# Cross-attention of a decoder layer: the order of a step, the grouping of the routing, and where the token scatters are issued

## The chip, the cores and the metric

One core of a Trainium2 chip runs one whole decoder layer. The metric is the device time in microseconds. The engines are TensorE (PE), VectorE (DVE), ScalarE (ACT), GpSimd (POOL) and SyncE (SP), which here only issues DMAs.

## The reference, cut to what matters

x is 16 sequences of 128 tokens, width 512; 16 heads of 32.

```
x1  = x + self_attention(layernorm(x))
d   = rs * (softmax(q(layernorm(x1)) . k(ctx) / sqrt(32), masked) . v(ctx) @ Wo.T + bo)
d   = (d - mean(d)) / sqrt(var(d) + 1e-5) * gamma + beta        # rs = clip(residual_scale, 0, 0.3)
x3  = x1 + d
xf  = layernorm(x3)
scores = softmax(xf @ gate.T)             # 64 experts in 8 groups; best 3 groups, of them best 6 experts
slot = expert * 192 + min(position of the token among those of its expert, 191)
out = x3 + sum_k weight_k * expert_k(xf) + shared_expert(xf)
```

A token beyond place 191 of its expert shares the last slot; the last token of the expert that got there holds it.

## The kernel before, in words

Four phases follow each other, with a barrier of all engines between them: self-attention, cross-attention (`cross_phase`), the routed experts, the shared expert. Only `cross_phase` and its helpers are changed.

**The work of the cross-attention.** One step t handles one sequence (a tile of 128 tokens). A quad is four tiles. All matrices are split in a high and a low part (`_hi`, `_lo`), and `matmul3` (L35) adds three products per chunk, so one projection unit is 12 matmuls of 512 columns. A quad has four key units, four V units (one per tile) and four query units; `cross_units` (L646) spreads the units of the next quad over four steps, three per step. ScalarE copies the key and query units out of PSUM, VectorE the V units. `cross_fresh` (L658) says which x tiles are turned in a step, `cross_context` (L666) which context tiles are split.

**A step**, in PE's order: scores of tile t (`scores`, L1484), the spreading of the inverse row sums of tile t-1 over the columns (`widen`, L1519), unit 0, transposes of x, unit 1, transpose of xf (`turn_final`, t-2), output projection (`project_out`, t-1), router logits (t-2), positions of a group, unit 2, row sums (`sums`, t) and V products (`attend_v`, t). VectorE: bound the scores in four pieces (`bounded`), with `attn_out(t-1)` (V products times inverse) between the second and third; units, statistics; `output(t-1)`; the row maximum of the logits; `delta(t-1)` (writes x3); the group's routing; `final_norm(t-1)` (writes xf); `row_sums(t)` (reciprocal). ScalarE: four exponentials, the copy of the spread inverse (`rinv_out`), the high part of the attention (`attn_hi`), unit copies, the high part of xf, the contexts' high parts, the router exponential. POOL: the low part of the attention (`attn_lo`, L960), the contexts' low parts, the addition of beta to the residual tile (`residual`), the inverse deviations of the next x tiles (`inv_std`), of the delta and of x3 (`delta_factor`, `final_rstd`), and the scatters.

**PSUM.** Two banks `pj` take the units and the output projection in turn. Two banks `ex` are shared by the small products; `cross_uses` (L680) writes down their order of use, and each use waits until the one before was read: `ex[1]` holds in turn the spread inverse, turned x, the logits, the positions and the row sums.

**Routing.** After the router, VectorE ranks the experts of a group of tiles (`rank_experts`, L1280), chooses six per token (`choose_experts`, L1308), and, after PE's running counts, computes the slots (`place_tokens`, L1334). `CROSS_GROUPS` (L642) has six groups of 4, 4, 3, 3, 1 and 1 tiles; `group_steps` (L674) gives their steps. Then POOL writes each token's number to its slots in a table in DRAM: `scatter` (L979) issues six indirect DMAs of 128 numbers per tile. `SCATTER_STEP` (L643) gives the step of each tile; the scatters stand at the end of POOL's step. The expert phase reads this table first, after the last scatter and a last small store (L930).

**Start-up.** The first six weight pieces were loaded during the self-attention. SP (from L898) loads contexts 0 and 1, three x tiles, the mask, contexts 2 and 3 (each waits for the low part of the context two before, in a ring of two buffers), then weights, x tile 3, weights, contexts 4 to 7. ScalarE's queue issues the seven loads of biases and vectors (L1051 to L1056). POOL waits for all seven (L1022), scales `bias_q`, then makes the low parts of contexts 0 to 3 with the inverse deviations of x tiles 0 to 3 between them, then `constants` (L987), then the low parts of contexts 4 to 7. PE turns one x tile after each of the four first key units, so x tile 3, which needs the buffer of tile 0, can be loaded after the first one.

In the loop SP issues, per step, the loads of x and contexts, the store of x3(t-1), the store of xf(t-1), and the load of the residual tile t+1 (`load_xr`, L882).

## Time and profile before

| | us |
|---|---|
| median of 3 runs | 1815.17 |
| lowest, highest | 1814.08, 1817.7 |
| the profiled execution | 1820.86 |
| its span, first to last instruction | 1819.1 |

| engine | busy us | share of the span |
|---|---|---|
| PE | 1556.5 | 86% |
| DVE | 1229.8 | 68% |
| ACT | 897.3 | 49% |
| POOL | 672.4 | 37% |

The time to predict is the median; the rows are those of the one profiled execution, and times in them count from the start of its span. "Busy" is the union of the instructions of an engine; a wait is shown before the instruction that waited, with what ended it. DMA issues stand under SPq or ACTq.

### The profile page before, as it was taken

What the parts mean: (1) busy time and instruction counts of PE and PEld (TensorE: products, weight loads), DVE (VectorE), ACT (ScalarE), POOL (GpSimd) and SP (SyncE); (2) the same over time, 40 slices, a digit from 0 to 9 for tenths busy, and PEclk for the clock granted to TensorE, in tenths of its full rate; (3) what the DMA queues carried; (4) which work ended last, traced back from release to release, by engine and by line L of the source; (5) the groups of instructions that cost most, each with busy time, mean ns of one, the idle gap of its engine ahead of it and who ended that gap; (6) DMA issues with size and microseconds to landing.
All of it is one profiled execution on the core that took longest, in us unless ns stands there. A gap on an engine that the chain in (4) does not pass through costs nothing. (4 is left out here: it accounts for less than half of the span.)

```text
span 1819.1 us, 30976 instructions
## 1 busy us (share of the span) xinstructions
PE 1556.5 (86%) x10503; PEld 1311.8 (72%) x10503; DVE 1229.8 (68%) x2130; ACT 897.3 (49%) x1748; POOL 672.4 (37%) x925
## 2 busy tenths in 40 slices
PE   5999987588878855309999999999999999799996
PEld 3788865477767644208888888888888888577774
DVE  5677664455666664527888888888888888454455
ACT  3566653333323221007777777777777777411110
POOL 1222221323226355553433444433333333323563
PEclk9999998799989976659999999999999999899998
DMA  5012111422113010029777777777777775424663
GB/s 179 18 42 76 36 36 35 144 71 69 53 53 51 27 47 24 18 91 349 260 256 258 252 253 261 256 256 250 261 253 248 262 253 206 154 70 146 200 185 104
DMA packets 110493, 275.71 MB, mean 152 GB/s; under 512 B 17696, under 2 KB 17792, under 8 KB 110416
## 3 DMA queue, kind: packets, MB, share of 16 engines
q1 hardware_dynamic: 88848, 222.65, 35.9%
q0 software_dynamic: 18464, 50.45, 8.7%
q10 hardware_dynamic: 3104, 1.58, 0.3%
q8 instruction: 48, 0.79, 0.2%
q14 instruction: 29, 0.24, 0.1%
HBM read 232.59 MB, written 42.04 MB: 151 GB/s over the span
## 5 line engine op out<-in xcount | busy, mean ns | idle before, releaser
L1784 POOL TENSOR_TENSOR e_hid<-e_h_raw,e_hid 128x192 fp32r<-128x192 f32 (+1 forms) x192 | 177.9, 926 | 410.9 <-ACT e_hid L1840 409.5
L1998 PE MATMUL e_gu<-e_xT_hi_lo,e_wg 128*128 128x384 f32 (+1 forms) x768 | 231.0, 357 | 2.1 <-issue 1.1
L1998 PE MATMUL e_gu<-e_xT_hi_lo,e_wu 128*128 128x384 f32 (+1 forms) x768 | 229.8, 355 | 0.0
L2000 PE MATMUL e_gu<-e_xT_hi_lo,e_wu 128*128 128x192 f32 (+1 forms) x768 | 193.5, 252 | 0.0
L2000 PE MATMUL e_gu<-e_xT_hi_lo,e_wg 128*128 128x192 f32 (+1 forms) x768 | 193.3, 252 | 0.0
L1911 DVE TENSOR_TENSOR e_total<-e_gu,e_low 128x384 f32<-128x384 f32 (+1 forms) x192 | 106.1, 553 | 105.7 <-ACT e_low L1835 105.7
L39 PE MATMUL e_dn<-e_wd,e_hid 128*96 128x512 f32 (+1 forms) x384 | 154.2, 402 | 0.1
L41 PE MATMUL e_dn<-e_wd,e_hid 128*96 128x512 f32 (+1 forms) x384 | 151.5, 395 | 0.0
L40 PE MATMUL e_dn<-e_wd,e_hid 128*96 128x512 f32 (+1 forms) x384 | 150.5, 392 | 0.0
L1998 PEld LDWEIGHTS e_gu<-e_xT_hi_lo,e_wg 128*128 128x128 f32 (+1 forms) x768 | 138.1, 180 | 7.3 <-DVE e_total L1911 1.3
L2000 PEld LDWEIGHTS e_gu<-e_xT_hi_lo,e_wg 128*128 128x128 f32 (+1 forms) x768 | 140.2, 183 | 1.5
L1998 PEld LDWEIGHTS e_gu<-e_xT_hi_lo,e_wu 128*128 128x128 f32 (+1 forms) x768 | 138.0, 180 | 3.4
L2000 PEld LDWEIGHTS e_gu<-e_xT_hi_lo,e_wu 128*128 128x128 f32 (+1 forms) x768 | 140.2, 183 | 0.0
L1899 DVE TENSOR_TENSOR e_wu<-e_raw_u,e_wu 128x1408 fp32r<-128x1408 f32 x64 | 127.6, 1994 | 0.1
L1904 DVE TENSOR_TENSOR e_wd<-e_raw_d,e_wd 128x1024 fp32r<-128x1024 f32 (+1 forms) x128 | 120.5, 941 | 0.0
L2160 POOL DMA_INDIRECT h_yk<-y_dram,h_idx x96 | 104.0, 1083 | 28.0 <-issue 24.1
L1840 ACT ACTIVATE e_hid<-e_h_raw 128x192 fp32r<-128x192 f32 (+1 forms) x192 | 69.2, 360 | 90.3 <-DVE e_h_raw L1920 90.3
L983 POOL DMA_INDIRECT table_dram<-c_token,c_wslot x96 | 93.5, 974 | 44.0 <-issue 27.5
L1816 ACT ACTIVATE e_wg<-e_raw_g 128x1408 fp32r<-128x1408 f32 x64 | 88.4, 1382 | 40.7 <-DMA e_raw_g<-in_L_ffn_Wg_dram 40.7
L1825 ACT ACTIVATE e_wd<-e_raw_d 128x1024 fp32r<-128x1024 f32 (+1 forms) x128 | 106.3, 831 | 0.0
L1899 DVE TENSOR_TENSOR e_wg<-e_raw_g,e_wg 128x1408 fp32r<-128x1408 f32 x64 | 103.4, 1616 | 3.5 <-ACT e_wg L1816 3.5
L1096 ACT ACTIVATE c_prT<-c_prT,c_not_bias,c_attend 128x512 f32<-128x512 f32 x64 | 50.9, 809 | 110.0 <-DVE c_prT L1226 110.0
(285 smaller groups left out, 4048.7 us busy)
## 6 DMA issues: line engine op xcount, KB each, us to landing
e_raw_g<-in_L_ffn_Wg_dram SPq DMA_DIRECT2D x64, 704.0 KB, 6.9
e_raw_u<-in_L_ffn_Wu_dram SPq DMA_DIRECT2D x64, 704.0 KB, 8.3
e_raw_d<-in_L_ffn_Wd_dram SPq DMA_DIRECT2D x64, 512.0 KB, 4.3
y_dram<-e_y SPq DMA_DIRECT2D x64, 384.0 KB, 7.0
e_raw_d<-in_L_ffn_Wd_dram SPq DMA_DIRECT2D x64, 192.0 KB, 4.6
s_x<-in_x_dram SPq DMA_DIRECT2D x16, 256.0 KB, 3.4
s_xr<-in_x_dram SPq DMA_DIRECT2D x16, 256.0 KB, 3.7
x_dram<-s_x SPq DMA_DIRECT2D x16, 256.0 KB, 2.1
```

The lines of the kernel that those rows point to most:

```text
L39: pe.matmul(out, al, bh, start=first, stop=False)
L40: pe.matmul(out, ah, bl, start=False, stop=False)
L41: return pe.matmul(out, ah, bh, start=False, stop=last)
L983: pool.indirect_dma_start(out=route["table"], in_=token[:, t:t + 1], in_offset=None, out_offset=bass.IndirectOffsetOnAxis(ap=wslot[:, at:a ...
L1784: pool.tensor_tensor(hid[b][1][0:n, c, :], h_raw[b][0:n, c, :], hid[b][0][0:n, c, :].bitcast(F32), ALU.subtract).then_inc(s_hl, 1)
L1825: act.activation(wd[b][0][0:rows, cs, :], raw_d[b][0:rows, cs, :], ACT.Copy).then_inc(s_dh[b], 1)
L1899: dve.tensor_tensor(w[b][1][:], raw[b][:], w[b][0][:].bitcast(F32), ALU.subtract).then_inc(s_gul[b], 1)
L1904: dve.tensor_tensor(wd[b][1][0:rows, cs, :], raw_d[b][0:rows, cs, :], wd[b][0][0:rows, cs, :].bitcast(F32), ALU.subtract).then_inc(s_dl[b], 1)
L1911: dve.tensor_tensor(total[0:n, c], gu[m][0:n, :, 0:CAP], low[m][0:n], ALU.add).then_inc(s_sum, 1)
L1998: pe.matmul(bank[0:n, 0:2 * CAP], w[b][0][:, k, m:m + n], xT[:, :, k, toks], start=k == 0, stop=False)
L2000: ins = pe.matmul(bank[0:n, 0:CAP], w[b][1][:, k, m:m + n], xT[:, 0, k, toks], start=False, stop=k == KC - 1)
L2160: pool.indirect_dma_start(out=yk[b][:, k * H:(k + 1) * H], out_offset=None, in_=y_in, in_offset=bass.IndirectOffsetOnAxis(ap=idx[b][:, k:k ...
```

## The change

It does the following in `cross_phase`:

- Order of the step. On PE, `sums(t)` and `attend_v(t)` come ahead of unit 2, and `widen(t)` behind it, at the end of step t (before: `widen(t-1)` behind the scores of step t). On VectorE, the four `bounded` come together, `final_norm(t-2)` behind them (before: `final_norm(t-1)` at the end of the step, so it moves over the step's edge), the group's routing ahead of `delta`, then `row_sums(t)`, unit 2, `attn_out(t)` and `attn_lo(t)`, which moves from POOL to VectorE. ScalarE does `rinv_out(t)` and `attn_hi(t)` at the end of step t.
- Routing in groups of two (the last two of one), each ranked and chosen in one step and placed in the next.
- Scatters in halves of three from step 4 on, one half at the start of POOL's step and one at its end; `SCATTER_STEP` goes.
- `delta_factor` has two instructions instead of four: with eps / rs^2 (a constant of VectorE, `delta_eps`) the factor 1 / sqrt(var + eps / rs^2) needs no product with rs.
- Start-up: four buffers for the first four contexts, two of them the residual tiles' (`ctx_at`), so that all four are loaded first; the low parts of contexts 0 and 2 go to VectorE; all loads of biases and vectors are issued by SP, in other places; PE turns x tiles behind the V units instead of the key units; the loads of weights and of contexts 4 to 7 are interleaved; the output weights are split behind the query units.

The diff, cut (what is not shown renames `XQ` to `PAIR` in the routing's buffers, passes a range to `scatter`, adds semaphores, writes the new order into `cross_uses`, adds `RS_MIN`, and makes the one-hot buffer two rows long):

```
...
-CROSS_GROUPS = ((0, 4), (4, 8), (8, 11), (11, 14), (14, 15), (15, 16))
-SCATTER_STEP = (7, 8, 9, 10, 11, 12, 13, 14, 14, 15, 15, 16, 16, 16, 17, 18)
+CROSS_GROUPS = ((0, 2), (2, 4), (4, 6), (6, 8), (8, 10), (10, 12), (12, 14), (14, 15), (15, 16))
+PAIR = 2
 DRAIN = 3
...
     last = CROSS_GROUPS[g][1] - 1
-    return (last + 2, last + 3, last + 4) if g < 3 else (last + 2, last + 2, last + 3)
+    return last + 2, last + 3
+
+
+def scatters(t, late):
+
+    if t >= BATCH:
+        return {16: [(12, 0, 6), (13, 0, 6)], 17: [(14, 0, 6)], 18: [(15, 0, 6)]}[t] if late else \
+            [(11, 3, 6)] if t == BATCH else []
+    half = 2 * (t - 4) + int(late) - 1
+    tile, part = divmod(half, 2)
+    return [(tile, 3 * part, 3 * part + 3)] if half >= 0 else []
...
+        def context_count(m):
+
+            return (m + 1) // 2 if m < CR else m - 1
+
+        def ctx_at(m):
+
+            return xb[m % 2][:] if 2 <= m < CR else ctx_sb[m % 2][:]
+
         before = STAGES
...
             def load_ctx(m):
-                if m >= 2:
-                    sp.wait_ge(s_cl, m - 1)
-                sp.dma_start(ctx_sb[m % 2][:], ctx_in[m * P:(m + 1) * P, :]).then_inc(s_c[m % 2], 16)
+                if m == CR:
+                    sp.wait_ge(s_cd, 1)
+                elif m > CR:
+                    sp.wait_ge(s_cl, context_count(m - 2))
+                sp.dma_start(ctx_at(m), ctx_in[m * P:(m + 1) * P, :]).then_inc(s_c[m if m < CR else m % 2], 16)
...
             def load_xr(t):
-                if t >= 2:
+                if t == 0:
+                    sp.wait_ge(s_cd, 2)
+                elif t == 1:
+                    sp.wait_ge(s_cl, context_count(3))
+                else:
                     sp.wait_ge(s_x3, t - 1)
...
-            load_ctx(0)
-            load_ctx(1)
+            for m in range(CR):
+                load_ctx(m)
+            sp.dma_start(bias_k[:], vecs[1].rearrange("(c p) -> p c", p=P),
+                         allow_slow_non_contiguous=True).then_inc(s_bk, 16)
             for m in range(XR):
                 load_x(m)
+            for n in range(before, 2 * KC):
+                load_w(n)
+            sp.dma_start(bias_q[:], vecs[0].rearrange("(c p) -> p c", p=P),
+                         allow_slow_non_contiguous=True).then_inc(s_bq, 16)
+            sp.dma_start(bias_v[:], vecs[2].partition_broadcast(P)).then_inc(s_bv, 16)
             sp.dma_start(imask[:], route["mask"]).then_inc(s_mask, 16)
-            load_ctx(2)
-            load_ctx(3)
-            for n in range(before, 3 * KC):
+            for n in range(2 * KC, 3 * KC):
                 load_w(n)
+            for src, dst in zip(vecs[3:], (bias_out, gamma, beta, rs)):
+                sp.dma_start(dst[:], src.partition_broadcast(P)).then_inc(s_vec, 16)
             load_x(XR)
-            for n in range(3 * KC, len(pieces)):
+            load_ctx(XQ)
+            load_ctx(XQ + 1)
+            for n in range(3 * KC, 3 * KC + STAGES):
                 load_w(n)
-            for m in range(XQ, 2 * XQ):
-                load_ctx(m)
+            load_ctx(XQ + 2)
+            load_ctx(XQ + 3)
+            for n in range(3 * KC + STAGES, len(pieces)):
+                load_w(n)
             load_x(XQ)
...
-                lk(pool.tensor_tensor(fac[:], mv2[:, 1:2], rs2[:], ALU.mult))
-                lk(pool.tensor_tensor(fac[:], fac[:], eps[:], ALU.add))
-                lk(pool.tensor_tensor(fac[:], fac[:], minus_half[:], ALU.pow))
-                pool.tensor_tensor(fac[:], fac[:], rs[:], ALU.mult).then_inc(s_fac, 1)
+                lk(pool.tensor_tensor(fac[:], mv2[:, 1:2], eps_rs[:], ALU.add))
+                pool.tensor_tensor(fac[:], fac[:], minus_half[:], ALU.pow).then_inc(s_fac, 1)
...
                 pool.dma_start(table, zero_row[:]).then_inc(s_zero, 16)
+                pool.wait_ge(s_vec, 16 * len(vecs[3:]))
                 lk(pool.tensor_scalar(rs[:], rs[:], 0.0, RES_MAX, ALU.max, ALU.min))
-                lk(pool.tensor_tensor(rs2[:], rs[:], rs[:], ALU.mult))
-                pool.memset(mark[:], 0.0).then_inc(s_const, 1)
-
-            pool.wait_ge(s_vec, 16 * len(vecs))
-            lk(pool.tensor_scalar(bias_q[:], bias_q[:], SCALE, None, ALU.mult))
+                lk(pool.tensor_tensor(rs[:], rs[:], rs[:], ALU.mult))
+                pool.tensor_scalar(rs[:], rs[:], RS_MIN, None, ALU.max).then_inc(s_const, 1)
+
+            pool.wait_ge(s_bq, 16)
+            pool.tensor_scalar(bias_q[:], bias_q[:], SCALE, None, ALU.mult).then_inc(s_bqs, 1)
+            context_lo(1)
+            context_lo(3)
             for m in range(XQ):
-                context_lo(m)
                 inv_std(m)
...
             for t in range(BATCH + DRAIN):
-                if 1 <= t <= BATCH:
-                    attn_lo(t - 1)
-                for m in cross_context(t):
-                    context_lo(m)
+                for b, k0, k1 in scatters(t, False):
+                    if t == 4:
+                        pool.wait_ge(s_zero, 16)
+                    scatter(b, k0, k1)
                 if t < BATCH:
...
                         inv_std(m)
+                for m in cross_context(t):
+                    context_lo(m)
                 if 1 <= t <= BATCH:
...
                     final_rstd(t - 1)
-                if t == min(SCATTER_STEP):
-                    pool.wait_ge(s_zero, 16)
-                for b in range(BATCH):
-                    if SCATTER_STEP[b] == t:
-                        scatter(b)
+                for b, k0, k1 in scatters(t, True):
+                    if t == 4:
+                        pool.wait_ge(s_zero, 16)
+                    scatter(b, k0, k1)
...
         def _(act):
-            act.dma_start(bias_k[:], vecs[1].rearrange("(c p) -> p c", p=P),
-                          allow_slow_non_contiguous=True).then_inc(s_vec, 16)
-            act.dma_start(bias_q[:], vecs[0].rearrange("(c p) -> p c", p=P),
-                          allow_slow_non_contiguous=True).then_inc(s_vec, 16)
-            for src, dst in zip(vecs[2:], (bias_v, bias_out, gamma, beta, rs)):
-                act.dma_start(dst[:], src.partition_broadcast(P)).then_inc(s_vec, 16)
-
             def split_hi(n):
...
-            context_hi(0)
-            context_hi(1)
             for n in range(KC):
                 split_hi(n)
-            context_hi(2)
-            context_hi(3)
+            for m in range(CR):
+                context_hi(m)
             for n in range(KC, 2 * KC):
                 split_hi(n)
-            act.wait_ge(s_vec, 16 * len(vecs))
+            act.wait_ge(s_bk, 16)
             for i in range(KC):
                 unit_out(("k", 0, i))
-                x_hi(i)
             for n in range(2 * KC, 3 * KC):
                 split_hi(n)
-            for n in range(3 * KC, len(pieces)):
-                split_hi(n)
-            act.wait_ge(s_pool, 3)
             for m in range(XQ):
+                x_hi(m)
                 context_hi(XQ + m)
+            act.wait_ge(s_bqs, 1)
             for i in range(KC):
                 unit_out(("q", 0, i))
+                split_hi(3 * KC + i)
+            for n in range(4 * KC, len(pieces)):
+                split_hi(n)
             act.wait_ge(s_att, 1)
...
                     exps(t, 0)
-                if 1 <= t <= BATCH:
-                    rinv_out(t - 1)
                 for u in late:
...
                     exps(t, 1)
-                if 1 <= t <= BATCH:
-                    attn_hi(t - 1)
-                if t < BATCH:
                     exps(t, 2)
...
                         unit_out(u)
+                if t < BATCH:
+                    rinv_out(t)
+                    attn_hi(t)
...
                 dve.tensor_tensor(lo, stage[:, n % STAGES, 0:m], hi.bitcast(F32), ALU.subtract).then_inc(s_lo, 1)
+
+            def context_lo(m):
+                cols = slice(m * P, (m + 1) * P)
+                dve.wait_ge(s_ch, m + 1)
+                dve.tensor_tensor(cT[1][:, :, cols], ctx_at(m).rearrange("p (k s) -> p k s", k=KC),
+                                  cT[0][:, :, cols].bitcast(F32), ALU.subtract).then_inc(s_cd, 1)
+
+            def attn_lo(t):
+                dve.wait_ge(s_ah, t + 1)
+                dve.tensor_tensor(aT[1][:].rearrange("p c s -> p (c s)"), attn[:],
+                                  aT[0][:].rearrange("p c s -> p (c s)").bitcast(F32), ALU.subtract).then_inc(s_al, 1)
+
+            def small_constants():
+                dve.wait_ge(s_mask, 16)
+                link(dve.tensor_scalar(attend[:], imask[:], 0.5, None, ALU.is_gt))
+                dve.tensor_scalar(not_bias[:], attend[:], 1.0, CLIP, ALU.subtract, ALU.mult).then_inc(s_att, 1)
+
+            def delta_eps():
+                dve.wait_ge(s_const, 1)
+                link(dve.reciprocal(eps_rs[:], rs[:]))
+                link(dve.tensor_scalar(eps_rs[:], eps_rs[:], LN_EPS, None, ALU.mult))
...
+            for n in range(KC):
+                split_lo(n)
+            context_lo(0)
+            context_lo(2)
+            for n in range(KC, 2 * KC):
+                split_lo(n)
             norm_stats(0)
             norm_stats(1)
-            for n in range(KC):
-                split_lo(n)
+            norm_stats(2)
             normed(0)
-            norm_stats(2)
             normed(1)
-            for n in range(KC, 2 * KC):
+            small_constants()
+            for n in range(2 * KC, 3 * KC):
                 split_lo(n)
             normed(2)
-            for m in range(XQ):
-                x_lo(m)
-                if m == 0:
-                    norm_stats(3)
-                if m == 1:
+            norm_stats(3)
+            dve.wait_ge(s_bv, 16)
+            for t in range(XQ):
+                unit_out(("v", t))
+                x_lo(t)
+                if t == 0:
                     normed(3)
-            dve.wait_ge(s_mask, 16)
-            link(dve.tensor_scalar(attend[:], imask[:], 0.5, None, ALU.is_gt))
-            dve.tensor_scalar(not_bias[:], attend[:], 1.0, CLIP, ALU.subtract, ALU.mult).then_inc(s_att, 1)
-            for n in range(2 * KC, 3 * KC):
-                split_lo(n)
-            for t in range(2):
-                unit_out(("v", t))
             for n in range(3 * KC, 4 * KC):
                 split_lo(n)
-            for t in range(2, XQ):
-                unit_out(("v", t))
             for n in range(4 * KC, len(pieces)):
...
             normed(XQ)
-            dve.wait_ge(s_const, 1)
+            delta_eps()
             for t in range(BATCH + DRAIN):
...
                 if t < BATCH:
-                    bounded(t, 0)
-                    bounded(t, 1)
-                if 1 <= t <= BATCH:
-                    attn_out(t - 1)
-                if t < BATCH:
-                    bounded(t, 2)
-                    bounded(t, 3)
+                    for j in range(HPC):
+                        bounded(t, j)
+                if 2 <= t < BATCH + 2:
+                    final_norm(t - 2)
                 for u in units[0:1]:
                     unit_out(u)
-                for g in range(NG):
-                    if group_steps(g)[1] == t and group_steps(g)[0] < t:
-                        choose_experts(g)
                 for m in ahead:
...
                     route_max(t - 2)
-                if 1 <= t <= BATCH:
-                    delta(t - 1)
                 for g in range(NG):
-                    if group_steps(g)[2] == t:
+                    if group_steps(g)[1] == t:
                         place_tokens(g)
...
                         rank_experts(g)
-                        if group_steps(g)[1] == t:
-                            choose_experts(g)
+                        choose_experts(g)
                 if 1 <= t <= BATCH:
-                    final_norm(t - 1)
+                    delta(t - 1)
+                if t < BATCH:
+                    row_sums(t)
                 for u in units[2:3]:
...
                 if t < BATCH:
-                    row_sums(t)
+                    attn_out(t)
+                    attn_lo(t)
             dve.tensor_copy(last_tok[:], last_tok[:]).then_inc(s_last, 1)
...
                     else:
-                        pe.wait_ge(s_cl, XQ * (q + 1))
+                        pe.wait_ge(s_cl, context_count(XQ * q + XQ - 1))
+                        pe.wait_ge(s_cd, 2)
                     cols = slice(i * P, (i + 1) * P)
...
                     scores(t)
-                if 1 <= t <= BATCH:
-                    widen(t - 1)
                 for u in units[0:1]:
...
                 for g in range(NG):
-                    if group_steps(g)[2] == t:
+                    if group_steps(g)[1] == t:
                         positions(g)
+                if t < BATCH:
+                    sums(t)
+                    attend_v(t)
                 for u in units[2:3]:
...
                 if t < BATCH:
-                    sums(t)
-                    attend_v(t)
+                    widen(t)
...
```

## Rows read from the trace of the kernel before

**Rows 1.** Busy time by stage: A, B, C, D, E of the cross-attention.
```profile
core 0: us, PE busy (x) PEld busy (x) DVE busy (x) ACT busy (x) POOL busy (x), PEclk, DMA share, GB/s
318.70:376.80 58.10, 36.59 (x160) 29.56 (x160) 26.48 (x50) 21.64 (x40) 22.40 (x44) 0.81 0.45 144
376.80:446.80 70.00, 63.88 (x637) 53.20 (x637) 37.86 (x76) 26.39 (x44) 20.30 (x34) 0.98 0.17 54
446.80:632.90 186.10, 157.52 (x1402) 131.62 (x1398) 123.39 (x321) 57.33 (x100) 69.42 (x108) 0.89 0.18 49
632.90:735.00 102.10, 51.70 (x539) 42.36 (x535) 61.99 (x186) 20.33 (x36) 53.02 (x68) 0.71 0.11 32
735.00:798.30 63.30, 14.67 (x65) 11.61 (x65) 26.26 (x110) 3.23 (x8) 37.70 (x43) 0.55 0.05 13
```

**Rows 2.** Waits, 446.8 to 735: waiting line, awaited line, total, times, longest.
```profile
PE c_ex L1522 <- DVE c_rinv L1233: 28.2, 10, 5.1
PE c_pj L39 <- POOL c_aT_lo L964: 14.4, 4, 7.5
```

**Rows 3.** Timeline of the start-up: start, us, engine, line, operation, [idle before, awaited].
```profile
328.65 0.78 POOL L1023 TENSOR_SCALAR c_bias_q<-c_bias_q 128x4 f32<-128x4 f32 x1 [9.74 <-DMA c_rs<-attn_residual_scale_dram]
...
337.64 0.76 PE L39 MATMUL c_pj<-c_cT_hi,c_wk_lo 128*128 128x512 f32 x1 [22.90 <-POOL c_cT_lo L953]
...
345.38 0.70 DVE L1198 BATCH_NORM_STATS2 c_stats<-c_x 128x6 f32<-128x512 f32 x1 [1.25 <-DMA c_x<-x_dram]
...
351.90 0.48 PE L39 MATMUL c_pj<-c_wv_hi,c_cT_lo 128*128 128x512 f32 x1
...
355.26 0.10 POOL L1020 MEMSET c_mark<- 128x1 f32 x1
...
362.89 0.39 PE L39 MATMUL c_pj<-c_xT_hi,c_wq_lo 128*128 128x512 f32 x1
```

**Rows 4.** Landing of the residual tiles' loads (256 KB each).
```profile
DMA to landing us min/median/max: 2.7/2.8/5.9
```

**Rows 5.** Timeline of step 16: from the last row sums to the last output.
```profile
735.00 0.95 DVE L1233 RECIPROCAL c_rinv<-c_ex 128x128 f32<-128x128 f32 x1
...
736.00 2.07 PE L1522 MATMUL c_ex<-c_rinv,c_spread 128*128 128x128 f32 x8 [10.05 <-DVE c_rinv L1233]
...
738.80 0.69 DVE L1240 TENSOR_TENSOR c_attn<-c_ex,c_rb 128x512 f32<-128x512 f32 x1 [2.85 <-issue]
...
742.40 1.28 POOL L964 TENSOR_TENSOR c_aT_lo<-c_attn,c_aT_hi 128x512 fp32r<-128x512 f32 x1
...
743.82 0.77 PE L39 MATMUL c_pj<-c_wo_hi,c_aT_lo 128*128 128x512 f32 x1 [3.10 <-POOL c_aT_lo L964]
...
748.35 0.69 DVE L1245 TENSOR_TENSOR stage<-c_pj,c_bias_out 128x512 f32<-128x512 f32 x1 [6.27 <-PE c_pj L41]
```

**Rows 6.** Timeline of VectorE: first and last rows of ranking, choice and placing.
```profile
725.98 0.14 DVE L1286 RECIPROCAL c_lsum<-c_lsum 128x3 f32<-128x3 f32 x1
...
734.54 0.54 DVE L1268 TENSOR_SCALAR stage<-c_x,c_fmv,c_rstd 128x512 f32<-128x512 f32 x1
...
753.88 0.52 DVE L1340 TENSOR_REDUCE c_lmax<-c_ex 64x3 f32<-64x384 f32 x1
...
759.08 0.16 DVE L1286 RECIPROCAL c_lsum<-c_lsum 128x1 f32<-128x1 f32 x1
...
763.39 0.54 DVE L1268 TENSOR_SCALAR stage<-c_x,c_fmv,c_rstd 128x512 f32<-128x512 f32 x1
```

**Rows 7.** Timeline of POOL: first and last of the 30 final scatters.
```profile
759.45 1.02 POOL L983 DMA_INDIRECT table_dram<-c_token,c_wslot  x1 [4.60 <-DVE c_wslot L1362]
...
796.13 0.96 POOL L983 DMA_INDIRECT table_dram<-c_token,c_wslot  x1 [0.31 <-issue]
```

**Rows 8.** POOL's residual addition, the cast beside it, and all casts of that line.
```profile
665.42 1.28 POOL L958 TENSOR_TENSOR c_xb<-c_xb,c_beta 128x512 f32<-128x512 f32 x1
665.80 0.94 DVE L1320 CAST c_tidf<-c_tidx 128x24 f32<-128x24 uint32 x1
...
L1320 DVE CAST c_tidf<-c_tidx 128x32 f32<-128x32 uint32 (+2 forms) x6 | 1.8, 305 | 0.2
```

81 lines of the change are left out of this document (39 added, 42 removed).

## The prediction

> **What bounds the kernel now.** I read the share of each stage first. The cross-attention stage runs from 318.7 to about 798.3 us of a 1819.1 us span [rows 1], and nothing of the diff acts outside it; the expert work behind it only starts earlier or later. I cut the stage into five: start-up A (318.7 to the first scores at 376.8), steps 0 to 3 (B), steps 4 to 11 (C), step 12 to the row sums of step 15 (D), and the tail E. In A to C TensorE (PE) is busy most of the time; in D and E it is busy half and a quarter, and its granted clock falls to 0.71 and 0.55. There the path is a chain that passes through all engines. The waits of PE [rows 2] name two: `widen`, put behind the scores, waits for the reciprocal on VectorE (28.2 us in C and D together), and the output projection waits for `attn_lo` on POOL (14.4 us, all in D), where `attn_lo` stands behind six or twelve scatters. In E POOL is the bound: it issues scatters without a gap from 759.45 on [rows 7].
>
> **A, start-up.** Two things pull against each other.
> Now POOL waits until 328.65 for seven small loads, then makes the low parts of four contexts and the inverse deviations between them; PE starts at 337.64 [rows 3]. The change loads four contexts at once and gives two low parts to VectorE, but POOL's first instruction waits for `bias_q`, issued on SP behind four contexts, `bias_k`, three x tiles and two weight pieces: nine transfers of 256 KB. At 300 GB/s (an estimate: twice the mean of A, 144 GB/s [rows 1], since A has long pauses) they need 7.9 us; with some 2 us to start and the narrow bias loads `bias_q` lands near 330, and PE starts at 330 + 0.8 + 2.5 = 333.4, 4.2 us earlier. The bounds: 327.5 (contexts last) and 335.
> Against it, the four key units come before any x transpose. The first transpose follows one V unit: 13 us for four key units (14.3 [rows 3], less their four transposes), 2.75 for one V unit (11.0 for four [rows 3]) and 0.4, so 16.3 us after PE's start instead of 4.4. It releases the load of x tile 3: 2.8 us to land [rows 4]. Then its statistics on VectorE and POOL's inverse and constants, 345.38 to 355.4 = 10.0 us [rows 3], then `context_lo(4)` (1.3), the load of context 6, which waits for it (2.8), its high part on ScalarE (0.6), and **only then** `x_hi(3)` (0.6), queued behind it, and `x_lo(3)` (0.7), for which every query unit waits. Sum 16.3 + 2.8 + 10.0 + 1.3 + 2.8 + 0.6 + 0.6 + 0.7 = 35.1 us. From the first query unit to the scores it is 13.9 us now [rows 3, 1]; after an idle of 7 us PE may run at the lower clock, so I take 14.2 for it. First scores: 333.4 + 35.1 + 14.2 = 382.7 against 376.8: **A +6 us** (0 to +8).
>
> **The loop of the steps.** The new order closes one ring per step: `row_sums(t)`, `widen(t)`, copy, `attn_out`, high part, `attn_lo` (now VectorE), four bounds of the next scores, then `final_norm`. Count from the start W of `widen`. To `attn_out` 1.9 us at the high clock, 2.8 at the low one (736.00 to 738.80 [rows 5]); `attn_out` 0.7, high part 0.7, low part 0.7, four bounds 2.5, norm 0.6: W + 7.0. A new wait stands here: SP's queue issues the store of that xf tile and, behind it, `load_xr`; before, the norm came at the end of the step before. So the residual lands at 7.0 + 0.8 + 2.8 [rows 4] = W + 10.6. Behind POOL's residual (1.3, the size of `attn_lo` [rows 5]) stands the inverse deviation of the next x tile (0.9), and VectorE's `normed` (0.6) stands in front of `output`: O, the start of `output`, is W + 12.9 to 13.7 with one or two fresh tiles, where PE would have had the projection ready at about W + 11.3 (scores, two units, transposes, projection: three times 2.75 and some 3 us).
> From O on all is VectorE. Output, factor and delta are 753.88 - 748.35 = 5.5 us [rows 5, 6]; the wait for the factor in it (1.4, which two of POOL's four instructions fewer would shorten) is hidden behind the group work, that for the exponent (0.6) is not: 4.7. A group of two costs the middle of one and three: ranking and choice (8.6 and 4.3) 6.4, placing 4.1 (5.2 for three, of which I keep a fixed 2) [rows 6]. Row sums 0.95. So O to W is 12.1 in odd steps, 10.2 in even ones (with positions). PE passes sums, V products and unit (4.8 us) in that time and then waits 2 to 5 us: **the unit put ahead of `widen` does not cover it**.
> Four steps: 13.7 + 10.2, 12.9 + 12.1, 11.3 + 10.2, 12.9 + 12.1 = 95.4 us. After each such wait PE's first unit and `widen` may run at the low clock (`widen` 2.07 us, a projection 4.5 instead of 3.0 [rows 5]); I add 3 us in four steps, from bounds of 0 and 8. **C**: 2 x 98.5 = 197 against 186.1 now [rows 1]: +11 (+4 to +20). **B**: groups start at step 3 (now 5) and the exponent's wait of 1 us a step is no longer covered by the unit; +1, +1, -1, +4 for steps 0 to 3: +5 (+2 to +7).
> **D**, without units: O is W + 7.9, a transpose (0.8) and a projection at the low clock (4.5) = W + 13.2; steps 12 to 15 are 23.3, 25.2, 23.3, 25.2 less 2.6 for the two ends of the stretch: 94.4 against 102.1 [rows 1]: **-8** (-18 to -3). What goes is POOL's scatters ahead of `attn_lo`; late next is VectorE.
> **E**: from the row sums at 735.00. `attn_lo` no longer waits for POOL (742.40) and is done at 740.9; with the norm and the transpose of tile 14 ahead, `output(15)` starts at 12.1 instead of 13.4. Then placing of two, ranking of one, and **delta last**: 12.1 + 2.9 + 4.2 + 4.3 + 2.4 = 25.9. POOL's twelve late scatters stand behind `final_rstd(15)` (0.9), so start at 27.0 although their slots are there at 19. Six scatters a tile at 1.265 us (29 intervals in 36.7 us [rows 7]): 24 of them, 30.4 us; last table store 1.2 later: 58.6 against 63.3: **-5** (-8 to 0).
> Parts costed at nothing: the bias loads' move from ScalarE's queue to SP's (hidden unless `bias_q` is late, above); half scatters of 3.8 us before the residual in the steady steps, which end before xr lands at W + 10.6; context low parts behind the inverse, whose factor has 5 us of room; smaller tiles of the routing.
> Sum: +6 + 5 + 11 - 8 - 5 = **+9 us**. The profiled execution took 1820.86 us around its span of 1819.1, which is 5.7 above the median of the three shown, 1815.17; against its own time 1830, against the median 1824.
>
> **A rule weighed.** The one cast of six that met POOL's residual addition took 0.94 us, against 0.17 for the other five (six times 305 ns in all); POOL's addition had started 0.4 us before [rows 8]. `attn_lo` on VectorE now meets scatters, not such additions; I price that at 0 and bound it by 0.8 a step. The Trainium skill (SBUF — State Buffer, "Who interferes with whom") says that a VectorE instruction with two SBUF inputs contends with a GpSimd instruction that reads SBUF and that the loser blocks for the whole instruction; by it each new `attn_lo` that meets a scatter would wait.
>
> **Rivals.**
> 1. *PE's clock stays high* (faster). The place is the ring after W: matmuls follow each wait in longer blocks. Then B is +3, C 191 (+5), D -18 and E -8 (`widen`, transpose and projection 3 us shorter [rows 5]): +6 + 3 + 5 - 18 - 8 = -12, 1803 us. It decides where D's granted clock passes about 0.9; for it speaks that B has 0.98, against it that PE has no more work in D than now, where it has 0.71 [rows 1]. 0.2.
> 2. *`bias_q` lands early*, at 324.5: PE starts at 327.5, limited by the contexts, and A is 0: 1818 us. For it: all seven loads of now were in at 328.65, with as many bytes ahead [rows 3]. 0.15.
> 3. *The scatters gain nothing*: POOL's last scatter ends as late after the row sums as now, since the last delta releases them: E 0, 1829 us. 0.1.
> 4. *The shared port*: 16 `attn_lo` at 0.8 each on the ring, +12: 1836 us, as is C at its upper bound. 0.1.
> Forecast: 0.45, its own range 1814 to 1832.
>
> **Numbers.** A measurement of this kernel can tell about 0.2% (3.6 us) from no change. Below 1811.5: rival 1 and a little of the others, 0.28. Between, 0.17: lower end of the forecast and part of rival 2. Above 1818.8: 0.55. The range, 1801 to 1838, takes in rivals 1 to 4.
>
> **What would show it.** First matmul near 333 and first scores near 383, with PE idle about 7 us ahead of the query units, and `context_hi(6)` right ahead of `x_hi(3)`. Scores of step 12 some 197 us after those of step 4, `widen` waiting up to 5 us for the reciprocal in odd steps, POOL's residual waiting for its DMA. No wait of the projection for `attn_lo`; from the last row sums to the table store 58 to 59 us. Wrong would be: scores(0) before 377, a C under 188, or a granted clock above 0.9 in D.

## The result and the profile after

The changed kernel takes 1845.46 us (median of 4 runs, 1837.29 to 1846.92) against 1816.43 for the kernel before beside it: ratio 1.0144, interval 1.0118 to 1.0171. The forecast was 1824 (1801 to 1838): the direction is right, the size is not, +29 us instead of +9. Profiled again later, it took 1838.68 us, ratio 1.0119 (1.0098 to 1.014): +24 us, still more than twice the forecast.

From the page of the changed kernel's profile (span, busy time, the granted clock in 40 slices; its profiled execution took 1846.92 us):

```profile
span 1845.2 us, 31021 instructions
PE 1573.5 (85%) x10506; PEld 1322.8 (72%) x10506; DVE 1252.6 (68%) x2228; ACT 898.8 (49%) x1748; POOL 643.8 (35%) x875
PEclk9999987799998986657999999999999999899998
```

The same five windows as in [rows 1], at this kernel's own stage limits (columns: us, then busy time of PE, PEld, DVE, ACT, POOL with the instructions, granted clock, DMA share, GB/s):

```profile
319.00:382.00 63.00, 41.56 (x165) 33.21 (x169) 22.84 (x43) 21.20 (x36) 17.57 (x39) 0.77 0.39 127
382.00:464.00 82.00, 68.32 (x644) 55.21 (x640) 52.89 (x125) 27.56 (x49) 18.27 (x30) 0.96 0.16 54
464.00:667.00 203.00, 161.57 (x1396) 133.68 (x1396) 138.30 (x388) 57.49 (x100) 75.41 (x101) 0.90 0.18 44
667.00:763.00 96.00, 55.18 (x533) 46.72 (x532) 58.04 (x172) 20.63 (x36) 32.62 (x41) 0.68 0.12 31
763.00:822.00 59.00, 14.88 (x63) 12.03 (x63) 26.36 (x111) 3.23 (x8) 31.49 (x36) 0.53 0.06 18
```

The granted clock is about what it was in [rows 1], 0.90 in C and 0.68 in D against 0.89 and 0.71, so these rows give the clock no visible part of the loss. What PE waits for in B to E (us in total, times, longest), to be held against [rows 2]:

```profile
PE c_ex L1557 <- DVE c_rinv L1276: 44.6, 13, 6.8
PE c_ex L48 <- DVE stage L1311: 31.2, 6, 12.5
PE c_ex L1540 <- ACT c_prob L1147: 15.7, 8, 4.3
PE c_ex L1540 <- DVE c_count L1387: 5.8, 6, 1.0
PE c_ex L1540 <- DVE c_xT_lo L1253: 2.4, 1, 2.4
```

The projection's wait for `attn_lo` (17.5 us before in the same stretch) is gone. `widen` (L1557) waits for the reciprocal about as much as before (42.6 us), and the row sums (L1540) now wait 23.9 us for exponent, counts and x low part, against 9.7 for exponent and counts. The transposes of xf (L48) wait 31.2 us for the normed tile, against 12.9: that wait is new in D.

Stage by stage, from the timelines of all runs told of below. A runs from SP's first context load to the first scores, E from the last reciprocal of the row sums to 2.2 us after the last scatter's start; "stage" is their sum. What each run changes is told in its own section.

| kernel | A | B | C | D | E | stage |
|---|---|---|---|---|---|---|
| before; again (e13) | 58.2; 58.2 | 70.0; 70.2 | 186.1; 185.9 | 102.1; 102.2 | 63.3; 63.4 | 479.7; 479.8 |
| forecast, as a difference | +6 | +5 | +11 | -8 | -5 | +9 |
| after; again (e14) | 62.8; 62.7 | 82.2; 82.3 | 203.5; 199.9 | 95.4; 95.4 | 58.6; 58.6 | 502.5; 498.9 |
| e1, residual's load ahead | 62.9 | 80.8 | 193.4 | 97.1 | 58.4 | 492.5 |
| e2, start-up of before | 59.9 | 78.0 | 201.5 | 94.2 | 58.6 | 492.2 |
| e3, order of before in part | 62.8 | 65.7 | 191.1 | 93.5 | 58.7 | 471.7 |
| e4, attn_lo on POOL | 62.7 | 78.5 | 191.2 | 90.7 | 58.4 | 481.4 |
| e7, widen and attn_out late | 62.8 | 76.4 | 193.0 | 91.1 | 58.7 | 482.0 |
| e8, unit 2 ahead of the sums | 62.8 | 80.8 | 217.1 | 107.4 | 58.5 | 526.6 |
| e5, e2 and e3 together | 60.3 | 63.5 | 192.7 | 93.9 | 58.4 | 468.7 |
| e15, e5 with attn_lo on POOL | 58.1 | 63.8 | 193.9 | 94.1 | 58.3 | 468.2 |
| e6, e5 with the load ahead | 60.3 | 63.1 | 182.2 | 93.6 | 58.7 | 457.9 |
| e9, e6 with attn_lo on POOL | 60.5 | 63.1 | 185.7 | 94.1 | 58.1 | 461.5 |
| e10, before, load ahead, attn_lo on VectorE | 60.2 | 68.4 | 190.5 | 107.4 | 65.0 | 491.4 |
| e11, before, load ahead | 60.3 | 68.4 | 197.1 | 107.9 | 68.0 | 501.7 |
| e12; again (e16), e6 with the tail | 60.1; 60.1 | 63.1; 63.1 | 181.4; 181.3 | 94.8; 94.8 | 55.1; 55.1 | 454.5; 454.4 |

What lies ahead of the stage (313.4 to 319.3 us) and behind it (1018.9 to 1024.4 us, in e5 to e9 and e12 1029 to 1039.7) moves from run to run with code that nobody changed. Between the two first profiles it gave +3.3 of the +26.1 us of span; the stage gave +22.8. Beside e5 to e12 the kernel before itself took 1847 to 1849 us (beside e5 to e8 on the same chip on which it had taken 1816.5 beside e1 to e4), so there I read the stages first and the ratio second.

Two microseconds of A are PE's clock. All eleven runs with the start-up of before have the first query unit 44.0 to 44.4 us behind the first context load, but A is 58.1 or 58.2 in three of them (before, e13, e15) and 59.9 to 60.5 in eight. Ahead of the third query unit PE waits 1.74 us in the kernel before, and its granted clock stays at 1.0. In e11 it waits 2.27 us, and the clock is then 0.5, the lower level of 1.2 GHz, for 3.4 us. Stretches behind that wait, of the kernel before and of e11 (columns as above):

```profile
370.00:376.00 6.00, 5.73 (x24) 4.43 (x24) 1.09 (x4) 1.45 (x3) 2.98 (x4) 1.00 0.31 112
368.00:371.00 3.00, 3.00 (x9) 2.31 (x8) 0.55 (x1) 0.00 (x0) 1.85 (x2) 0.50 0.32 124
```

So a difference of 2 us in A between two runs with that start-up says nothing of their edits.

**Start-up**, from the timeline (start, duration, engine, line; in brackets the idle time before and its releaser), to be held against [rows 3]:

```profile
328.98 0.28 POOL L1053 TENSOR_SCALAR c_bias_q<-c_bias_q 128x4 f32<-128x4 f32 x1 [9.68 <-DMA c_bias_q<-in_L_xattn_bq_dram]
...
332.26 0.77 PE L40 MATMUL c_pj<-c_cT_hi,c_wk_lo 128*128 128x512 f32 x1 [17.12 <-POOL c_cT_lo L991]
...
365.87 0.63 ACT L1096 ACTIVATE c_cT_hi<-c_ctx 128x512 fp32r<-128x512 f32 x1 [5.55 <-DMA c_ctx<-in_ctx_dram]
367.86 0.76 PE L40 MATMUL c_pj<-c_xT_hi,c_wq_lo 128*128 128x512 f32 x1 [4.98 <-DVE c_xT_lo L1253]
```

All four stand near where the forecast put them: bias_q near 330, PE's start near 333, the high part of context 6 ahead of `x_hi(3)`, PE idle ahead of the query units (4.98 us where 7 were forecast).

**The ring of a step**, step 5, timelines of SP, POOL and VectorE:

```profile
493.40 0.34 SPq L923 DMA_DIRECT2D xf_dram<-stage  x1
493.78 0.43 SPq L912 DMA_DIRECT2D c_xb<-x_dram  x1
494.26 3.07 SPq L896 DMA_DIRECT2D c_x<-x_dram  x2
...
500.96 1.26 POOL L996 TENSOR_TENSOR c_xb<-c_xb,c_beta 128x512 f32<-128x512 f32 x1 [6.72 <-DMA c_xb<-x_dram]
503.06 0.55 DVE L1247 TENSOR_SCALAR c_x<-c_x,c_mv,c_rstd 128x512 f32<-128x512 f32 x1 [4.13 <-POOL c_rstd L984]
503.52 0.68 DVE L1288 TENSOR_TENSOR stage<-c_pj,c_bias_out 128x512 f32<-128x512 f32 x1
```

`widen` started at W = 486.6 here. The load of the residual leaves at W + 7.2, somewhat ahead of the forecast (7.8), but between the store of xf and two loads of x it lands only at W + 14.3, not W + 10.6. POOL's addition starts right behind it, and `output` starts at W + 17.0 instead of 12.9 to 13.7.

### The profile page after: what moved, and what is told of

Read it like the earlier page. It is cut to its first block and busy times, and to the rows that moved or that the text cites. A ratio compares the mean times of both kernels' runs of the same rounds, so it can differ in the third digit from the quotient of the medians.

```text
span 1845.2 us, 31021 instructions
## 1 busy us (share of the span) xinstructions
PE 1573.5 (85%) x10506; PEld 1322.8 (72%) x10506; DVE 1252.6 (68%) x2228; ACT 898.8 (49%) x1748; POOL 643.8 (35%) x875
## 5 line engine op out<-in xcount | busy, mean ns | idle before, releaser
L2035 PE MATMUL e_gu<-e_xT_hi_lo,e_wg 128*128 128x192 f32 (+1 forms) x768 | 193.0, 251 | 0.0
L2195 POOL DMA_INDIRECT h_yk<-y_dram,h_idx x96 | 103.2, 1075 | 27.8 <-issue 24.1
L1865 ACT ACTIVATE e_act_g<-e_total 128x192 f32<-128x192 f32 (+1 forms) x192 | 70.1, 365 | 69.9 <-DVE e_total L1946 63.6
L1807 POOL DMA_INDIRECT e_xg<-xf_dram,e_idx x96 | 94.7, 987 | 25.6 <-issue 19.5
```

The costliest lines, as they stand in the source:

```text
L1807: pool.indirect_dma_start(out=xg[:, j * H:(j + 1) * H], out_offset=None, in_=xf, in_offset=bass.IndirectOffsetOnAxis(ap=idx[:, j:j + 1], a ...
L2035: ins = pe.matmul(bank[0:n, 0:CAP], w[b][1][:, k, m:m + n], xT[:, 0, k, toks], start=False, stop=k == KC - 1)
L2195: pool.indirect_dma_start(out=yk[b][:, k * H:(k + 1) * H], out_offset=None, in_=y_in, in_offset=bass.IndirectOffsetOnAxis(ap=idx[b][:, k:k ...
```

## The experiments

Ratios are to the kernel before of the same comparison.

**e1_xr_ahead.** The residual's load leaves with delta(t), ahead of both stores.

```
@@ store(t), on SP
                 sp.wait_ge(s_x3, t + 1)
+                if t + 2 < BATCH:
+                    load_xr(t + 2)
                 sp.dma_start(out_x[...], x3[t % 2][:])...
                 sp.wait_ge(s_xf, t + 1)
```

> The changed kernel (1845.5 us), but SP's queue issues the load of the residual tile t+2 as soon as delta(t) is out, ahead of both stores and of the wait for the normed tile, instead of behind them. Theory (the residual's ring): the load now leaves only behind final_norm, together with two or three other transfers, and lands 4 to 7 us later instead of 2.8; VectorE's waits for the next inverse deviation behind it are 11.7 us in steps 3 to 10. They go, and with them the same time of B and C: 1833 us (1829 to 1837), C near 192 instead of 203.5, no wait of POOL's residual for its DMA. Rival (the order of PE): PE had been waiting for the exponent anyway and the row sums wait for it as long as now: 1842 us or more, C above 200.

Measured: 1837.5 us, ratio 1.0131 (1.0109 to 1.0153); C 193.4, that is 10.1 less. POOL's groups in stage C (count, busy us, mean ns, idle ahead), first of the changed kernel:

```profile
L996 POOL TENSOR_TENSOR c_xb<-c_xb,c_beta 128x512 f32<-128x512 f32 x8 | 10.3, 1289 | 40.5 <-DMA c_xb<-x_dram 40.5
```

and of this run:

```profile
L996 POOL TENSOR_TENSOR c_xb<-c_xb,c_beta 128x512 f32<-128x512 f32 x8 | 10.3, 1294 | 1.4 <-DMA c_xb<-x_dram 1.2
```

The kernel before, in its own stage C, has no such wait at all:

```profile
L958 POOL TENSOR_TENSOR c_xb<-c_xb,c_beta 128x512 f32<-128x512 f32 x8 | 10.3, 1286 | 0.0
```

It is a wait that the change made: SP issues this load behind the store of xf, which waits for `final_norm`, and the change moved `final_norm` over the step's edge. 40.5 us of waiting in eight steps are gone in e1, and C gives back what the theory said; D does not (+1.7), because there `output` waits for PE. The stage is 10.0 shorter, the median 8.0: a little outside the 1829 to 1837 of the theory, well off the rival.

**e2_start_before.** Loads, engines and order of the start-up as in the kernel before.

```
-            for m in range(CR):
-                load_ctx(m)
+            load_ctx(0)
+            load_ctx(1)
...
-            for i in range(KC):
-                unit(("k", 0, i))
-            pe.wait_ge(s_lo, 2 * KC)
-            for t in range(XQ):
-                unit(("v", t))
-                turn_x(t)
+            for i in range(KC):
+                unit(("k", 0, i))
+                turn_x(i)
+            pe.wait_ge(s_lo, 2 * KC)
+            for t in range(XQ):
+                unit(("v", t))
```

> The changed kernel (1845.5 us) with the start-up of the kernel before: its order of loads on SP, its small loads on ScalarE's queue, four context low parts on POOL, transposes between the key units. Theory (start-up and the step behind it): stage A gives back 5.0 us and step 0 another 6, because the weight pieces, x tiles 4 to 6 and the statistics of tile 4 no longer arrive late: 1834.5 us (1832 to 1838), first scores at 377, step 0 of 12 to 13 us. Rival (only A belongs to the start-up; step 0 is long because routing and the new order begin there): 1840.5 us, step 0 still 17 to 18 us. Second rival (what starts earlier waits later, in C): within 2 us of 1845.

Measured: 1828.98 us, ratio 1.0074 (1.0057 to 1.0091). The scores of steps 0 and 1 on PE (the stage starts at 313.6 in this run):

```profile
373.51 1.17 PE L1522 MATMUL c_sc<-c_qT,c_kT 32*128 32x128 f32 x32 [0.87 <-ACT c_qT L1104]
386.48 1.17 PE L1522 MATMUL c_sc<-c_qT,c_kT 32*128 32x128 f32 x32
```

Step 0 takes 13.0 us instead of 18.1: against this run the late start-up costs 2.9 in A and 5.1 in step 0, and 10.3 in the whole stage. A gave back less than the 5.0 expected because this run has the 3.4 us at the lower clock told of above. The theory of step 0 holds; the median moved further (16.5 us, below the 1832 to 1838 expected), of which 5.4 lie ahead of the stage. What the changed start-up leaves behind for step 0 is in the timelines of SP and VectorE of the changed kernel:

```profile
374.83 2.99 SPq L917 DMA_DIRECT2D stage<-n_L_ffn_gate_weight_dram  x2
377.86 1.38 SPq L896 DMA_DIRECT2D c_x<-x_dram  x3
383.35 0.69 DVE L1241 BATCH_NORM_STATS2 c_stats<-c_x 128x6 f32<-128x512 f32 x1
385.22 1.50 DVE L1247 TENSOR_SCALAR c_x<-c_x,c_mv,c_rstd 128x512 f32<-128x512 f32 x1 [0.96 <-POOL c_rstd L984]
387.01 2.48 DVE L1269 TENSOR_SCALAR c_prT<-c_sc 128x512 f32<-128x512 f32 x4
```

The last gate pieces wait on SP's queue for the splitting between the query units and hold back x tiles 4 to 6; so statistics and normalisation of tile 4 stand in front of the bounds, which start 5.2 us after the scores (381.80).

**e3_order_before.** The places of unit, row sums, V products, `widen`, `attn_out` and `attn_hi` as before; `attn_lo` stays on VectorE, behind the bounds. Two parts of the changed order stay, here and in every run below that puts "the order" back: `final_norm(t-2)` behind the bounds of the next step, and the group's routing ahead of `delta`.

```
@@ PE (ScalarE and VectorE likewise)
                     scores(t)
+                if 1 <= t <= BATCH:
+                    widen(t - 1)
...
-                if t < BATCH:
-                    sums(t)
-                    attend_v(t)
                 for u in units[2:3]:
                     unit(u)
                 if t < BATCH:
-                    widen(t)
+                    sums(t)
+                    attend_v(t)
```

> The changed kernel (1845.5 us) with the order of the kernel before on PE, ScalarE and VectorE: third unit, then row sums and V products; the inverse's spreading behind the next scores; attn_out and attn_lo between and behind the four bounds. Theory (the residual's ring): the order is a smaller part; the unit covers the exponent's wait again (the row sums' waits for the exponent and the counts fall from 21.5 us to about 10), and the spreading waits behind the scores instead: C 195 to 202, D 2 to 8 us longer, in all 1838 to 1848. Rival (the order of PE is what made B and C longer than forecast): C and B lose 20 us: 1826 us or less.

Measured: 1812.87 us, ratio 0.9988 (0.9971 to 1.0004). PE's waits in B to E of this run:

```profile
PE c_ex L1564 <- DVE c_rinv L1279: 49.4, 14, 7.3
PE c_ex L1547 <- ACT c_prob L1148: 5.7, 4, 2.3
PE c_ex L1547 <- DVE c_count L1390: 1.9, 2, 1.0
```

The stage is 30.8 us shorter: B 16.5, C 12.4, D 1.9. The ring theory's share of the order, at most 7.5 us, was far too small; the rival's, at least 20 in B and C, is right in size (28.9). The median fell below both expectations (1838 to 1848; 1826 or less). Which wait it was, the sums do not say: those of the row sums fall from 23.9 to 7.6 us, that of `widen` grows by 5. The next three runs tell.

**e4_lo_on_pool.** `attn_lo` of the changed kernel back on POOL.

```
                     attn_out(t)
-                    attn_lo(t)
@@ POOL
             for t in range(BATCH + DRAIN):
+                if 1 <= t <= BATCH:
+                    attn_lo(t - 1)
                 for b, k0, k1 in scatters(t, False):
```

> The changed kernel (1845.5 us) with attn_lo back on POOL, at the head of each step ahead of the three early scatters. Rival of the shared port: VectorE's attn_lo contends with POOL, 0.8 us a step: moving it away gives back up to 12 us: 1834 us. Theory (no port cost: the sixteen attn_lo of the changed kernel took 0.69 us each): nothing comes back but 0.7 us a step of VectorE; against it attn_lo takes 1.26 us on POOL and may stand behind three late scatters of 3.8 us; most of that is hidden in B and C, and D gets 0 to 8 us longer: 1842 to 1855.

Measured: 1820.77 us, ratio 1.005 (1.0018 to 1.0082); the stage is 21.1 us shorter. `attn_lo` in the changed kernel (minimum, median and maximum ns, first and last start; under it what its engine waited for ahead of it):

```profile
L1226 DVE TENSOR_TENSOR c_aT_lo<-c_attn,c_aT_hi x16: 692/693/694, 402.1 to 768.1; 128x512 fp32r<-128x512 f32 x16
  ACT c_aT_hi L1134: 11.2, 16
```

No instance is stretched, so there is no port cost, yet the gain is one that only the rival had named. The price is the place: 16 x 0.69 us of work and 11.2 us of waiting for the high part, 22.3 us together, stand in front of the bounds of the next scores, and nearly all of it comes back. My own reading (only 0.7 us a step, mostly hidden; 1842 us or more) is refuted.

**e7_widen_late.** Half of e3: `widen` behind the next scores, `attn_out` between and `attn_lo` behind the bounds; row sums and V products stay ahead of unit 2. Three operations move here, not one.

```
@@ VectorE (PE and ScalarE as in e3)
                     bounded(t, 0)
                     bounded(t, 1)
+                if 1 <= t <= BATCH:
+                    attn_out(t - 1)
                     bounded(t, 2)
                     bounded(t, 3)
+                if 1 <= t <= BATCH:
+                    attn_lo(t - 1)
```

> Half of the order put back in the changed kernel: the inverse's spreading behind the next scores, attn_out between the bounds and attn_lo behind them, as in the kernel before; row sums and V products stay ahead of the third unit. Theory (VectorE's part of the ring is the cost: with the spreading at the end of the step, attn_out, the wait for the high part and attn_lo, 2.1 us, stand ahead of the bounds, and the bounds ahead of exponents and sums): most of the 32.6 us of the whole order come back, 20 to 30: 1815 to 1826. Rival (the uncovered wait of the row sums for the exponent, 21.5 us in all, is the cost): it stays, so at most 8 us come back: 1837 or more.

Measured: 1834.85 us, ratio 0.9942 (0.9893 to 0.9991); the stage is 20.5 us shorter, within the 20 to 30. The median is not in the 1815 to 1826: behind the stage this run took 16 us more than the changed kernel (1039.7 against 1023.7), in code that nobody changed. This row of PE's waits shows that the rival falls:

```profile
PE c_ex L1547 <- ACT c_prob L1148: 16.9, 8, 5.4
```

The row sums wait for the exponent as long as before (15.7), and the time came back all the same.

**e8_unit_first.** The other half: unit 2 ahead of row sums and V products, `widen` at the end.

```
+                for u in units[2:3]:
+                    unit(u)
                 if t < BATCH:
                     sums(t)
                     attend_v(t)
-                for u in units[2:3]:
-                    unit(u)
                 if t < BATCH:
                     widen(t)
```

> The other half: third unit ahead of row sums and V products again, the spreading straight behind them at the end of the step, so that PE waits for the reciprocal with nothing to do. Theory (VectorE's part of the ring): the waits of the row sums for exponent and counts shrink from 21.5 us, but PE waits some 1.5 us a step for the reciprocal, so -6 to +12: 1839 to 1857. Rival (the uncovered wait of the row sums is the cost): 15 to 25 us come back: 1820 to 1830.

Measured: 1874.34 us, ratio 1.0137 (1.0082 to 1.0191) to a kernel before of 1848.55; the stage is 24.1 us longer, twice the upper end of what I expected.

```profile
PE c_ex L1557 <- DVE c_rinv L1276: 66.6, 16, 7.8
PE c_ex L1540 <- ACT c_prob L1147: 2.0, 2, 1.0
PE c_ex L1540 <- DVE c_count L1387: 1.9, 2, 1.0
```

The row sums' wait is nearly gone (3.9 us of 23.9), `widen` waits 22 us longer, and with it the next scores. Given the late `widen`, the unit ahead of it is worth some 1.5 us a step in this kernel; it was the half of the order that did good there.

**e5_start_and_order and e15_routing_alone.** e5 puts back the start-up and what e3 puts back of the order; e15 also `attn_lo` (as in e4). e15 is thus the kernel before with

```
-CROSS_GROUPS = ((0, 4), (4, 8), (8, 11), (11, 14), (14, 15), (15, 16))
+CROSS_GROUPS = ((0, 2), (2, 4), (4, 6), (6, 8), (8, 10), (10, 12), (12, 14), (14, 15), (15, 16))
```

the scatters in threes, the short factor, and the two parts of the order that e3 leaves: the late `final_norm` and the routing ahead of `delta`. Its name says less than it holds.

> The changed kernel with both the start-up and the order on PE, ScalarE and VectorE of the kernel before: what is left of the change is routing in twos, attn_lo on VectorE, scatters in threes, and the shorter delta factor. Theory (the order and the start-up cost each by itself, the rest gains): against the run with the order alone put back (1812.9 us) the start-up gives back 3 us in stage A and less than 3 in step 0, which is 13.7 us there already: 1808 us (1803 to 1811), 0.3 to 0.7% under the kernel before (1816.5), D near 93 and the tail near 58.5 as in the changed kernel. Rival (the two are one effect, the exponents of step 0): within 2 us of 1812.9. Second rival (routing in twos loses in C what D and the tail gain): 1814 us or more, C above 194.

> The kernel before with the routing in twos, the scatters in threes and the short delta factor alone: start-up, order, attn_lo on POOL and the residual's load as before. Against e9_old_order_lo_pool, which has the residual's load ahead in addition (stage 461.5 us). Theory (attn_lo behind three scatters instead of twelve, and slots that are there earlier, are what shortens D and the tail): stage 468 to 474, D 93 to 97 against 102.1, tail 58 to 60 against 63.3, C 190 to 197. Rival (twos cost more on VectorE than they save): stage 478 or more.

Measured: e5 1822.24 us, ratio 0.9838 (0.9788 to 0.9888), above the 1803 to 1811 expected, with 1037.0 us behind the stage, and with a stage of 468.7, 3.0 under e3; e15 1809.59 us, ratio 0.9973 (0.996 to 0.9987), with 468.2, inside the 468 to 474. What is left of the change in e15 is the gain: against e13 11.6 us of stage, D 8.1 and E 5.1 shorter, B 6.4 shorter (steps 2 and 3), C 8.0 longer. No run parts the routing in twos and the scatters in threes from the late `final_norm`, the routing ahead of `delta` and the short factor, so which of them brings it was not shown. That the late `final_norm` has a price shows in POOL's residual addition in stage C of e15, which the kernel before did without waiting:

```profile
L980 POOL TENSOR_TENSOR c_xb<-c_xb,c_beta 128x512 f32<-128x512 f32 x8 | 10.3, 1292 | 10.2 <-DMA c_xb<-x_dram 10.2
```

Moving `attn_lo` to VectorE in the old order changes little (468.7 against 468.2, of which A has 2.2 from the clock as above). With the order put back the start-up costs 3.0, not 10.3: the two amplify each other in step 0.

**e6_start_order_xr and e9_old_order_lo_pool.** e5 with the load of e1, and that with `attn_lo` on POOL.

> The kernel of the run before (start-up and order put back) with the residual's load ahead of both stores. Theory (the residual's ring is the same in either order): the changed kernel gained 8 us by this; in the old order C has less slack on VectorE and PE, so 4 to 8 us less than the run before it: about 1802 us. Rival (the wait was a wait of the new order alone, which starts final_norm and the bounds late): nothing, within 2 us of the run before it.

> The run e6_start_order_xr (start-up and order of before, residual's load ahead; stage 457.9 us) with attn_lo on POOL at the head of each step. Theory (in the old order attn_lo is behind the bounds, so off VectorE's ring; on POOL it stands behind at most three scatters): C within 3 us of 182, D 0 to 6 us longer than 93.6, because POOL takes 1.26 us instead of 0.69 and meets scatters: stage 458 to 466, ratio to the kernel before 0.980 to 0.990. Rival (the shared port, or VectorE's load, counts here as in the changed kernel, where moving it gained 21 us): stage 445 or less.

Measured: e6 1809.1 us, ratio 0.9754 (0.9692 to 0.9816), stage 457.9: 10.8 less than e5, nearly all in C, more than the 4 to 8 I gave it, though the median missed the 1802 expected. The residual's wait is there with `widen` early or late, since both kernels keep the late `final_norm`. e9 1813.09 us, 0.9825 (0.9782 to 0.9868), stage 461.5 as expected, 3.6 longer than e6: the 21 us of e4 belong to the new order alone.

**e10_before_lo_vector_xr and e11_before_xr.** The kernel before with the load of e1; in e10 `attn_lo` on VectorE behind the bounds too.

> The kernel before (stage 479.7 us) with two edits: attn_lo on VectorE behind the bounds, and the residual's load ahead of both stores; its groups of four, three, one and its whole-tile scatters stay. Theory (attn_lo behind POOL's six or twelve scatters is what made D long): D gets 6 to 10 us shorter (92 to 96 against 102.1), the tail stays at 61 to 63.3, C as in the run with the load alone plus 0 to 5: stage 460 to 470. Rival (the routing in twos and scatters in threes, not attn_lo's place, brought D's gain): D 99 or more.

> The kernel before with the one edit that gained 10 us of C in the changed kernel and 10.8 with the old order: the residual's load ahead of both stores. Theory (the ring of the residual is there in the kernel before too, in its steps without ranking): B and C 5 to 11 us shorter (C 176 to 182 against 186.1), D and tail as before: ratio 0.994 to 0.997. Rival (in the kernel before final_norm ends the step before, so the load was early enough): C 185 or more, ratio within 0.002 of 1.

Measured: e10 1841.99 us, ratio 0.9998 (0.9969 to 1.0027); e11 1844.38, 0.9992 (0.9956 to 1.0027). No gain: both theories miss (stage 460 to 470; C 176 to 182). Against e11, e10 has D 0.5 shorter, and both are above the 99 of the rival; e15 had the 8 us of D with `attn_lo` on POOL. So the engine of `attn_lo` is not needed for D's gain. The stages (491.4, 501.7) are long for another reason, too, PE in e11 in step 10:

```profile
612.24 0.77 PE L1515 MATMUL c_ex<-c_prT,c_v 128*32 128x128 f32 x17
613.32 0.42 PE L1515 MATMUL c_ex<-c_prT,c_v 128*32 128x128 f32 x4 [0.31 <-issue]
616.22 0.38 PE L1515 MATMUL c_ex<-c_prT,c_v 128*32 128x128 f32 x2 [0.99 <-issue]
617.65 0.81 PE L1496 MATMUL c_sc<-c_qT,c_kT 32*128 32x128 f32 x4 [0.64 <-issue]
```

Thirty-two V products that take 1.1 us elsewhere take 4.4 here (five rows of the view, three of them shown), with pauses for which the profile shows no releaser. Such pauses add up to about 7 us in e10 and 8 in e11, less than the 11.7 and 22.0 by which their stages are longer; the rest is not explained. What the load ahead is worth in the kernel before can be read without them: its residual addition has no wait to give back (0.0 in the row under e1), because `final_norm(t-1)` ends the step before there, as the rival of e11 said. Step 4 was 2.9 us shorter, later steps longer.

**e13_before_again and e14_after_again.** The two kernels of the case, unchanged, profiled side by side, to tell the change from what moves by itself.

> The kernel before, unchanged, profiled beside the three runs after it, because its median moved from 1816 to 1848 us between the first four experiments and the rest. Theory (a stretch of its instructions is supplied late, as PE's idle time of 0.3 to 1.0 us between two matmuls of one group in e11 and e10 shows, 3.5 us at 612 to 619 and 5 us at 712 to 723): the stage is longer than 479.7 us by 5 to 22 us, in steps 10 to 14, with such gaps. Rival (only the expert work behind the stage moved, by 3 to 16 us, as in e5 to e9): stage 478 to 482, everything else behind it.

> The changed kernel, unchanged, beside it. Theory (the stage of the changed kernel has no such gaps): stage 500 to 505 as at first; against the kernel before of the same call the ratio is 1.000 to 1.008 if that kernel's stage is longer by the gaps, and 1.012 to 1.016 if it isn't.

Measured: 1817.69 us, ratio 1.0005 (0.9986 to 1.0023), and 1838.68, 1.0119. The kernel before was back at its first time, stage 479.8 and without such pauses, so whether they made its 1848 us earlier could not be seen; what it shows is that its stages repeat to 0.2 us. The changed kernel repeats in every stage but C, 3.6 us shorter, which puts its stage at 498.9, just under the 500 to 505 expected: its steps 5 and 7, where the residual's load meets two other loads, took 28.0 and 26.4 us instead of 29.9 and 28.2.

**e12_tail and e16_tail_again.** e6 with six of the last scatters ahead of the last `final_rstd`, the inverse deviation of x3.

```
@@ POOL
                     delta_factor(t - 1)
+                    if t == BATCH:
+                        scatter(12, 0, 6)
                     final_rstd(t - 1)
```

> The run e6_start_order_xr (stage 457.9 us, tail 58.7) with the six scatters of tile 12 ahead of the last final_rstd on POOL instead of behind it. Theory (the tail is 27 us of VectorE's work, behind which POOL issues 24 scatters at 1.265 us, although the slots of tiles 12 and 13 are there at 19): six scatters, 7.6 us, move into the gap: the tail is 51 to 53 us, the stage 450 to 453, ratio under that of e6 by 0.003 to 0.004. Rival (the scatters then delay final_rstd, final_norm and the exponent of tile 15, and the slots of tile 15 come too late): tail 57 or more.

> The run e12_tail again, with more rounds, in the same call as the two kernels of the case: stage 452 to 457. Against the kernel before of this call 0.975 to 0.988, and under the changed kernel by 44 to 50 us. If its advantage is the noise of one call, the ratio comes to 0.99 or more.

Measured: e12 1797.52 us, ratio 0.9742 (0.9705 to 0.9779); e16 1793.56, ratio 0.9871 (0.985 to 0.9892) to a kernel before of 1814.66, and 45.1 us under the changed kernel. The tail is 55.1 instead of 58.7, half of the 7.6 and between theory (51 to 53) and rival (57). POOL in e16, the first scatters of tiles 13, 14 and 15 and the last of all:

```profile
745.88 1.28 POOL L996 DMA_INDIRECT table_dram<-c_token,c_wslot  x1 [0.20 <-issue]
...
756.20 0.96 POOL L996 DMA_INDIRECT table_dram<-c_token,c_wslot  x1 [2.71 <-DVE c_wslot L1399]
764.28 0.96 POOL L996 DMA_INDIRECT table_dram<-c_token,c_wslot  x1 [0.82 <-DVE c_wslot L1399]
770.59 0.96 POOL L996 DMA_INDIRECT table_dram<-c_token,c_wslot  x1 [0.30 <-issue]
```

POOL now waits for the slots of tiles 14 and 15: VectorE has become the tail's bound. This version beats both kernels (1.3% under the kernel before).

## Why the prediction was wrong

**A, +6: right** (+4.6), through the steps named. (The first transpose is 16.15 us behind PE's start by its terms, not 16.3.)

**B, +5: the first term that was mis-sized** (+12.2). The step that failed is "+1, +1, -1, +4 for steps 0 to 3": they were +6.2, +2.8, -2.4 and +5.6. Step 0 is 5.2 of the 7.2 us missed: I had followed the start-up only up to the first scores and costed the rest of its queue at nothing. Behind the first scores SP's queue, the splits and the statistics of tile 4 were late too, and in the new order all of it stands ahead of the bounds. e2 and e3 each shorten step 0 by 4 to 5 us; they do not add up.

**C, +11: the second** (+17.4). The step that failed is "the residual lands at 7.0 + 0.8 + 2.8". In steps 4 to 11 POOL's addition starts at W + 9.9, 14.4, 12.2, 11.7, 12.0, 10.3, 11.2 and 11.6, after the landing each time, and `output` at W + 14.1 in the mean where the sum had 12.7: 1.4 us in each of eight steps, 11.4. About half a microsecond a step of this is my adding: 10.6 + 1.3 + 0.9 + 0.6 is 13.4 for one fresh tile, not 12.9. The way from `output` to the next `widen` came out as forecast, 11.2 against 11.2, in part by luck: the terms of an even step add up to 9.8, I took 10.2, and 10.1 to 10.7 were measured. The 6 us that I had added for PE's clock were not needed and covered part of the miss. In the repeat (e14) C is +14.0 against e13, with the longest landing 5.9 us instead of 7.1, and the miss is 3 us instead of 6.4; so the size of this second term, unlike that of B, moves by half from one profile to the next. The 2.8 us were the landing of a load that leaves alone [rows 4]; this one leaves between a store and up to two loads. e1 removes that wait and C shrinks by 10.1. The term of the wrong size is the 2.8 for the landing: the eight loads of stage C took 2.7 to 7.1 us, 3.9 in the median.

**A sentence of the text was half right**: "the unit put ahead of `widen` does not cover it". In the odd steps of C PE still waited 3.4 to 4.8 us for the reciprocal, as forecast, in the even ones 0 to 1.7; but the unit covers part of it, for e8 takes it away and loses 24 us. And the forecast had not priced the order as a part by itself: e3 shows that it costs 30.8 us, e4 and e7 that two thirds of them hang on `attn_lo` and its wait ahead of the bounds. My ring had them in (W + 7.0), so its sum was near; I did not see that the order costs more than the whole loss, and that the rest of the change gains.

**D, -8, and E, -5: right** (-6.7, -4.7; the tail 58.6 as forecast). For D the reason is half wrong: the wait of the projection for `attn_lo` goes, as forecast, but it also goes in e15 with `attn_lo` on POOL, behind at most three scatters; so scatters of three are enough for it, and the engine is not needed. Whether groups of two, the late `final_norm` or the routing ahead of `delta` has a part in D and E stays open. Behind and ahead of the stage I had put nothing; +3.3 of the profiled difference lie there, and repeats of unchanged code move as much.

**The rivals.** PE's clock did not stay high (0.68 in D); bias_q was not early; the tail did gain. The shared port did not act on `attn_lo`, though twelve of its sixteen instances overlapped a scatter. (By its own terms C at its upper bound gives 1833 us, not the 1836 written there.) The range ended at 1838 because C's upper bound, +20, was never added to B's and A's: A 8, B 7, C 20, D -3, E 0 would have been +32.

## What to carry to other kernels

Before moving an operation to the end of a step, list what then stands in front of the next step's first work on each engine: here an operation of 0.69 us with a wait of 0.70 ahead of it, off the ring before, cost 21 us in sixteen steps. A load's landing time from a row holds only for the company it was measured in; if an edit makes it leave together with others, take the slowest landing of such a burst, and ask first whether it can leave earlier. Ask also what the operation that you move released: here the norm's move put the residual's load on the ring, where the kernel before had no wait for it. A start-up is not priced at its first product: follow its queue until the steady step.

## What the runs showed of the hardware

- A load of 256 KB landed in 2.8 us in the median in the kernel before [rows 4] and in 7.1 us between a store and two loads (issued at 493.78 above, the addition that waits for it starts at 500.96), while SP's issue of those two loads itself took 3.07 us.
- In the start-up of before, PE's granted clock stayed at 1.0 behind a wait of 1.74 us and was 0.5 for 3.4 us behind one of 2.27 us; nine matmuls take 3.00 us there (rows above), and A is 2 us longer in the eight runs where it happens.
- `normed` on VectorE took 0.52 to 0.55 us in eleven of its sixteen instances (two more: 0.69 and 1.10) but 1.50, 1.48 and 1.49 us at 385.22, 449.46 and 553.04, each 0.05 to 0.07 us behind the start of an addition or subtraction on POOL. A subtraction of VectorE with both inputs in SBUF did the same once: the last of these four starts at 329.3, 0.07 us behind POOL's, and took 1.74 us instead of 0.69 (first the group with its shortest, median and longest time in ns, then POOL's instruction):

```profile
L1216 DVE TENSOR_TENSOR c_wv_lo<-stage,c_wv_hi x4: 684/693/1737, 325.2 to 329.3; 128x512 fp32r<-128x512 f32 x4
329.23 1.25 POOL L991 TENSOR_TENSOR c_cT_lo<-c_ctx,c_cT_hi 128x512 fp32r<-128x512 f32 x1
```

`attn_lo`, also with both inputs in SBUF, stayed at 0.69 all 16 times; twelve of them overlapped a scatter of POOL, none an addition or subtraction. The Trainium skill (SBUF — State Buffer, "Who interferes with whom") says that a `tensor_scalar` may take the port pair that VectorE shares with GpSimd, and that whoever comes second waits for the whole instruction; by that rule the trace agrees for `normed`, and the subtraction at 329.3 agrees with what the prediction quotes of that section for two inputs in SBUF.
- In e10 and e11 PE paused 0.3 to 1.0 us between products of one group, without a releaser, while the kernel before took 1847 us; its own two profiles, taken when it stood at 1815 to 1818 us, show none. The cause stays open.
